# Reciprocal roots by a GpSimd power, and new instruction lists, in a cross-attention and expert kernel

## The reference

```python
x = x + xcond(layernorm(x), ctx, ctx, k_length)      # 8 heads of 16 channels; softmax over 256 keys,
                                                     # scores scaled by SCALE * log(k_length)
x = x + ffn(layernorm(x), w_router, w_fc, w_proj)    # x_flat: (1024, 256)
# layernorm(v) = (v - mean(v)) / sqrt(var(v) + 1e-5), over the last axis
# ffn: logits = x_flat @ w_router.T; the better of 2 experts is chosen, weighted by its softmax
#      h = x @ w_fc[e].T (1024 hidden); a = leaky(h, 0.5) ** 2; out = a @ w_proj[e].T
```

## Time and profile before

| | |
|---|---|
| median of three runs | 172.73 us |
| span of the profiled execution | 170.4 us (the page gives no other time of it) |
| TensorE busy | 161.4 us (95%) |
| VectorE busy | 129.2 us (76%) |
| ScalarE busy | 97.0 us (57%) |
| GpSimd busy | 58.6 us (34%) |
| chain that ended last, by engine | PE 75%, DVE 11%, waits not shown 4%, SP's queue 3%, ACT 3%, DMA 2% |

### The profile page before, as it was taken

One profiled execution on the slowest core, in us unless ns is written; L12 is line 12 of the kernel. 1 busy time (PEld: TensorE's weight loads), 2 busy tenths in 40 slices (PEclk: granted clock), 3 DMA queues, 4 the chain that ended last, 5 costly groups with the idle time before them and its releaser, 6 DMA issues.

```text
span 170.4 us, 4075 instructions
## 1 busy us (share of the span) xinstructions
PE 161.4 (95%) x1494; PEld 139.9 (82%) x1494; DVE 129.2 (76%) x301; ACT 97.0 (57%) x181; POOL 58.6 (34%) x68
## 2 busy tenths in 40 slices
PE   7998887899999989999989999999999999999992
PEld 7986745487698869896978798969879999999991
DVE  7799987999898999995999867953179875056442
ACT  4444979558659956957346526943794065335220
POOL 7331544630322420372521260405023253136330
PEclk9999999999999999999999999999999999999999
DMA  4577857794468054004501460002010000010001
GB/s 120 167 241 246 259 190 233 217 292 126 143 229 251 3 161 120 14 19 139 174 0 62 125 189 4 0 0 67 0 62 0 4 0 0 4 61 0 0 4 62
DMA packets 18883, 16.98 MB, mean 100 GB/s; under 512 B 1776, under 2 KB 18672, under 8 KB 18864
## 3 DMA queue, kind: packets, MB, share of 16 engines
q1 hardware_dynamic: 18144, 16.00, 30.3%
q10 hardware_dynamic: 720, 0.73, 1.5%
HBM read 8.72 MB, written 1.05 MB: 57 GB/s over the span
## 4 chain that ended last, share of the span: by engine, by line
PE 75%; DVE 11%; issue 4%; SPq 3%; ACT 3%; DMA 2%; DVEq 0%; ACTq 0%
PE hp L1358 25%; PE ops L1388 22%; PE pv L1342 6%; PE stp L1318 6%; PE ops L1273 5%; DVE negm L813 5%; PE snp L1265 3%; DMA x_raw<-x 2%; ACT probs L514 2%; DVE a_lo L921 2%; PE ops L1376 2%; PE pv L1376 1%; PE stp L1324 1%; PE pv L1398 1%; PE snp L1301 1%
## 5 line engine op out<-in xcount | busy, mean ns | idle before, releaser
L378 POOL TENSOR_TENSOR a_buf<-l_buf 128x512 f32<-128x512 f32 x32 | 35.7, 1119 | 77.8 <-DVE a_lo L921 44.6
L514 ACT ACTIVATE probs<-stp,scale_b 128x1024 f32<-128x1024 f32 x30 | 33.4, 1114 | 14.8 <-PE stp L1318 11.3
L1358 PE MATMUL hp<-xt_hi,wfc_hi 128*128 128x256 f32 x128 | 37.2, 291 | 0.0
L813 DVE TENSOR_REDUCE negm<-snp 128x4 f32<-128x1024 f32 x28 | 34.1, 1218 | 3.6 <-PE snp L1265 3.4
L1358 PE MATMUL hp<-xt_hi,wfc_lo 128*128 128x256 f32 x128 | 35.8, 279 | 0.0
L1358 PE MATMUL hp<-xt_lo,wfc_hi 128*128 128x256 f32 x128 | 35.7, 279 | 0.0
L522 ACT ACTIVATE l_buf<-hp 128x512 f32<-128x512 f32 x32 | 18.8, 594 | 23.7 <-PE hp L1358 17.0
L921 DVE TENSOR_TENSOR a_lo<-a_buf,a_hi 128x512 fp32r<-128x512 f32 x32 | 26.2, 831 | 7.6 <-ACT a_hi L529 6.2
L1358 PEld LDWEIGHTS hp<-xt_hi,wfc_hi 128*128 128x128 f32 x128 | 24.0, 188 | 2.1 <-issue 1.0
L1388 PE MATMUL ops<-wproj_hi,a_hi 128*128 128x256 f32 x112 | 23.6, 292 | 0.5 <-DVE wproj_lo L953 0.5
L1358 PEld LDWEIGHTS hp<-xt_hi,wfc_lo 128*128 128x128 f32 x128 | 24.1, 188 | 0.0
(11 more groups left out here) (112 smaller groups left out, 237.2 us busy)
## 6 DMA issues: line engine op xcount, KB each, us to landing
k_st<-k_hi SPq DMA_DIRECT2D x16, 128.0 KB, 2.1
wfc_raw<-w_fc_t SPq DMA_DIRECT2D x8, 256.0 KB, 4.4
wproj_raw<-w_proj_t SPq DMA_DIRECT2D x8, 256.0 KB, 3.5
q_st<-q_hi SPq DMA_DIRECT2D x14, 128.0 KB, 2.1
x_raw<-x SPq DMA_DIRECT2D x8, 128.0 KB, 3.0
k_st<-k_lo SPq DMA_DIRECT2D x8, 128.0 KB, 2.4
v_raw<-ctx_t SPq DMA_DIRECT2D x8, 128.0 KB, 2.6
x_keep<-x SPq DMA_DIRECT2D x8, 128.0 KB, 2.7
```

The source lines that it names most:

```text
L378: pool.tensor_tensor(a_buf[d % 2][:, :, :], l_buf[d % 2][:, :, :], l_buf[d % 2][:, :, :], ALU.mult).then_inc(s_a, 1)
L514: act.activation(probs[g][:, :, :, :], pair[:, :, :].rearrange("p e (c n) -> p e c n", c=KC), ACT.Exp, scale=scale_b[:, b:b + 1]).then_inc ...
L813: dve.tensor_reduce(negm[b % 2][:, :, :, g].rearrange("p c e -> p e c"), pair[:, :, :].rearrange("p e (c n) -> p e c n", c=KC), AX.X, ALU. ...
L1358: last = pe.matmul(hp[:, d % 2, half], wfc[w][:, kc, c * P:(c + 1) * P], xt[:, kc, :], start=(c % 2 == 0 and kc == 0 and w == 0 and xt is ...
```

## The change

The reciprocal root is now one GpSimd instruction per batch: (variance + eps) to the power -0.5, with a column `expo` that VectorE fills with -0.5 at the head. The logarithms, exponentials and Newton steps are gone. The lists of all five engines are written in another order. ScalarE's table load stands at the head of its list in both kernels.

```diff
-            def x_ln(b):
-                act.wait_ge(s_xvar, b + 1)
-                act.activation(xln[b % 2][:, :], xvar[b % 2][:, :], ACT.Ln, scale=-2.0).then_inc(s_xln, 1)
-
-            def x_rstd(b):
-                act.wait_ge(s_xln, b + 1)
-                act.activation(xrs[b % 2][:, :], xln[b % 2][:, :], ACT.Exp, scale=-0.5).then_inc(s_xrs, 1)
...
-                if stage == 0:
-                    dve.wait_ge(s_rs_, b + 1)
-                    dve.scalar_tensor_tensor(n1[:, :], rs[:, :], rs[:, 0:1], var[:, :], ALU.mult, ALU.mult).then_inc(s_n1_, 1)
-                else:
-                    dve.wait_ge(s_n1_, b + 1)
-                    dve.scalar_tensor_tensor(sc[:, :], n1[:, :], 1.5, rs[:, :], ALU.add, ALU.mult).then_inc(s_sc_, 1)
...
+            def x_scale(b):
+
+                j = b % 2
+                if b == 0:
+                    pool.wait_ge(s_expo, 1)
+                pool.wait_ge(s_xvar, b + 1)
+                wait(pool, s_qf, b - 1)
+                pool.tensor_tensor(xsc[j][:, :], xvar[j][:, :], expo[:, :], ALU.pow).then_inc(s_xsc, 1)
+
+            def y_scale(b):
+
+                j = b % 2
+                pool.wait_ge(s_yvar, b + 1)
+                wait(pool, s_x2n, b - 1)
+                pool.tensor_tensor(ysc[j][:, :], yvar[j][:, :], expo[:, :], ALU.pow).then_inc(s_ysc, 1)
...
-                    dve.tensor_scalar(var[:, :], mv[:, 1:2], EPS, -0.5, ALU.add, ALU.mult).then_inc(s_var_, 1)
+                    wait(dve, s_used, b - 1)
+                    dve.tensor_scalar(var[:, :], mv[:, 1:2], EPS, None, ALU.add).then_inc(s_var_, 1)
...
             load_x(sp, 0)
             load_x(sp, 1)
+            load_weights(sp, 0, 0)
+            load_weights(sp, 0, 1)
+            load_v(1)
             stack_k(sp, 0, 0)
```

More of the change, by code:

```diff
@@ L72, in build @@
         xst, xmv, xvar = two("xst", [P, 6]), two("xmv", [P, 2]), two("xvar", [P, 1])
-        xln, xrs, xn1, xsc = (two(n, [P, 1]) for n in ("xln", "xrs", "xn1", "xsc"))
+        xsc, expo = two("xsc", [P, 1]), sb("expo", [P, 1])
         q_f = two("q_f", [P, DIM])
@@ L87, in build @@
         yst, ymv, yvar = two("yst", [P, 6]), two("ymv", [P, 2]), two("yvar", [P, 1])
-        yln, yrs, yn1, ysc = (two(n, [P, 1]) for n in ("yln", "yrs", "yn1", "ysc"))
+        ysc = two("ysc", [P, 1])
         dot_out = sb("dot_out", [P, DIM])
@@ L383, in _ @@
             zero_k(0)
[L384 to L389, removed]
             fill_sel(0)
             fill_sel(1)
+            x_scale(0)
+            x_scale(1)
+            zero_nm(0)
             split_k(1)
+            split_k(2)
+            fill_v(0)
+            zero_k(1)
+            place_v(0)
+            fill_v(1)
+            place_v(1)
+            zero_nm(1)
+            x_scale(2)
             split_w(0, 0)
-            place_v(0)
-            split_k(2)
+            x_scale(3)
             split_w(0, 1)
             split_w(0, 2)
+            make_zeros()
             split_w(0, 3)
+            x_scale(4)
+            x_scale(5)
             split_k(3)
-            place_v(1)
+            split_k(4)
+            y_scale(0)
+            place_v(2)
+            place_v(3)
+            y_scale(1)
+            split_k(5)
             split_w(0, 4)
@@ L427, in _ @@
             square(1, 5)
+            y_scale(4)
+            y_scale(5)
+            place_v(7)
             square(1, 6)
@@ L741, in _, with fill_expo, moments @@
         def _(dve):
-            def moments(stage, b, src, st, mv, var, s_st_, s_mv_, s_var_):
+            def fill_expo():
+                dve.memset(expo[:, :], -0.5).then_inc(s_expo, 1)
+            def moments(stage, b, src, st, mv, var, s_st_, s_mv_, s_var_, s_used):
                 if stage == 0:
@@ L1078, in _ @@
-            x2_sum(2)
-            row_max(4, 1)
-            square_lo(0, 1)
-            x2_moments(2, 0)
+            q_part_lo(5)
+            split_max_lo(3)
+            x_moments(6, 1)
+            split_w_lo(1, 0)
+            split_w_lo(1, 1)
+            split_w_lo(1, 2)
+            split_w_lo(1, 3)
+            split_w_lo(1, 4)
+            square_lo(0, 0)
+            x_moments(6, 2)
+            pv_turn(2)
+            row_max(4, 0)
+            den_inverse(2)
+            attention_out(2)
@@ L1082, in _ @@
+            row_max(4, 1)
+            attention_turn(2)
+            x2_sum(2)
+            neg_logit(0)
+            x_moments(7, 0)
+            neg_abs(0)
+            row_max(4, 2)
+            square_lo(0, 1)
+            row_max(4, 3)
+            split_max_hi(4)
+            split_max_lo(4)
+            x2_moments(2, 0)
+            x_moments(7, 1)
             x2_moments(2, 1)
             coef_sum(0)
-            row_max(4, 2)
+            x2_moments(2, 2)
+            x_moments(7, 2)
@@ L1484, in _ @@
             scores_qk(3, 1)
+            x_transpose(0)
             warm(48)
-            x_transpose(0)
             scores_kq(2, 2)
+            warm(49)
             scores_qk(3, 2)
-            warm(49)
             ffn1(0, 0)
@@ L1494, in _ @@
             values(2, 0)
-            values(2, 1)
             ffn1(0, 2)
```

760 lines of the change are left out of this document (330 added, 430 removed).

## The result

| | before | after |
|---|---|---|
| median, us | 172.91 (172.65 to 173.48, four runs) | 177.53 (175.75 to 179.67, four runs) |
| profiled execution, us | span 170.4 | 177.23, span 175.4 |
| TensorE, VectorE, ScalarE, GpSimd busy, us | 161.4, 129.2, 97.0, 58.6 | 163.1, 129.2, 93.2, 67.7 |

The changed kernel is slower, by a ratio of 1.0231 (95% interval 1.0176 to 1.0285). The forecast had the sign right and was 2.9 us too low; the median lies 0.5 us above its range. By the ratio the time would be 176.9 (1.0231 times 172.91), just inside it.

What follows compares the result with a forecast made beforehand. Latency was taken to bound the kernel up to 41.94 us, TensorE's fixed stock of work after that. Head +1.0, middle +0.3, shape changes +1.6 and waits -1.0 summed to +1.9, so 174.6 us, range 171.7 to 177.0.

Steps and rivals of the forecast that it cites:

- the one from q to the last maximum: Opening: q 1.63 us late, less savings, makes batch 0's last maximum 1.04 late, priced +1.0 us (+0.6 to +5.2).
- two savings: Opening: q_lo of batch 1 moved ahead of the first maxima saves 0.35 us, one warm fewer between permutations 0.24.
- Constants: Start of q: constants land later because SP issues weights and v first; taken as 0.1 us, bounds 0 and 2.5.
- The ISA row: Start of q: a row before GpSimd's first two-input instruction costs between 0 and 0.98 us; taken as 0.1.
- The power: Start of q: one GpSimd power on one column, estimated at 0.35 us from the sizes of other GpSimd instructions.
- the rival of 1.28: Opening: the power takes as long as GpSimd's dearest instruction, adding 1.4 us, so 176.0 us; chance 0.12.
- the code load: Opening: the first power pays its own code load, 175.5 us or more, about 180 by the skill's figure; chance 0.04.
- The place that was priced: Middle, batch 2: first to second scores about 2.2 us, second to fourth maximum 3.9; the middle's net was +0.3.
- The waits: Long stretch: TensorE's named waits of 0.49 us (split maxima) and 0.54 (weight piece) both regained, -1.0 us.
- The changes of shape: Long stretch: 16 more TensorE tile shape changes at 0.10 us each, +1.6 us, bounds 0 and 3.0.
- Faster: Opening: VectorE's throughput is the limit there, so removed instructions give back 1.9 us; 171.8 us, chance 0.18.
- no change: Whole kernel: head +0.6, middle 0, shape changes +0.8, waits -1.0, together +0.4, so 173.1 us; chance 0.14.

Runs made afterwards that it cites:

- c: Changed kernel with ten more warm calls (20 multiplications of zeros) ahead of the first permutation; 175.81 us, ratio 1.019 to the kernel before.
- a: Changed kernel with SP's two early weight pieces and early piece of v put behind batch 0's k stack transfers; 173.79 us, ratio 1.0064 to the kernel before.
- d: Changed kernel with SP's early loads moved back, first power ahead of the casts and q_part_lo(0) ahead of q_normalise(1); 174.76 us, ratio 1.0085.
- e: Changed kernel with loads back, power ahead of casts, VectorE's batch 0 statistics ahead of k's low part, q_f(0) before batch 1's statistics; 174.46 us, ratio 1.007.
- t: Changed kernel with early loads moved back and the first half of values right ahead of the second in batches 2 to 7; 176.53 us, ratio 1.0215.
- m: Changed kernel with early loads moved back and TensorE's list up to the first projection in the order of the kernel before; 175.78 us, ratio 1.0161.
- p2: Kernel before, old lists with the power, plus batch 4's max_transpose one chunk later and two weight pieces' low parts earlier on VectorE; 171.0 us, ratio 0.9864.
- p: Kernel before with its own lists, only the reciprocal roots replaced by GpSimd powers, the first ahead of the casts; 171.84 us, ratio 0.9937.
- b: Changed kernel with the first power ahead of GpSimd's two casts and q_part_lo(0) ahead of q_normalise(1) on VectorE; 175.06 us, ratio 1.0098.
- q: New lists on all engines with the old reciprocal root (logarithm, exponential, Newton pair), no power on GpSimd; 183.08 us, ratio 1.0492 to the kernel before.
- pi: Old lists with the power, without the seven warm calls between batch 0's second and third scores; 172.39 us, ratio 0.9951 to the kernel before.
- pl: Old lists with the power, but SP issues two weight pieces and one of v ahead of batch 0's k stacks; 172.79 us, ratio 0.9972.

## Why the prediction was right in sign and wrong in size

**Slower: right, for a reason that is half of the true one.** The power does wait for the constants and the casts. But q's lateness was expected to pass through at its own size, and it did not. Against the landmarks the head was priced 3.66 too low, the middle 0.82 too low and the long stretch 1.32 too high. That the time came out near the upper bound and not far above it is luck: the third miss hid part of the first two.

**The step that failed is the one from q to the last maximum.** It put q 1.63 late (it was 2.27, 7.31 for 5.04) and let the maxima follow at their old pace, less two savings, "1.04 late". It took TensorE's pace as given and never asked what TensorE does while q is late. It idles, and the granted clock falls to the lower of its two levels (1.2 for 2.4 GHz). The head came out at +4.66. The runs, read one after the other by the first transpose, part it so (one profiled execution each, and a step's size depends on this order; c's added zeros are not in a): 2.76 the clock (changed kernel to c), 0.61 the early loads (c to a), 0.22 the power behind the casts (a to d), 0.37 statistics behind k (d to e), 0.70 left over the kernel before, by the row at ScalarE's copy of q.

The Trainium skill, TensorE: Matmul & The Clock Gate, Part 1, "What's actually happening", says that the slow clock is the default state and that activity releases the throttle. The stage rows above agree: 0.77 and then 0.71 behind the idle time, and c, where zeros fill it, has 1.00 in both stages up to 20 us. They do not show when idle time is enough: t's 1.55 us and m's 2.01 were followed by no fall. Read against the planned gap ahead of the permutation, that rule would have given this rival.

**The terms of q's start.** Constants: +0.70 in place of 0.1 (5.92 for 5.22). The bound of 2.5 had the mechanism, transfers that share the engines; a shows it. What the step left out is that the k stacks share them too (4.66 us in the chain; 2.1 before). The ISA row: 0.04 (6.68 to 6.72) for 0.1. The power: 0.55 for 0.35; the rival of 1.28 falls, and so does the code load.

The Trainium skill's 6 us for a first call (GPSIMD Engine Reference, section 2.1 "Instruction dispatch") do not show here: the first power starts 0.04 us after the cast ends.

**Middle: +1.12 for +0.3.** The place that was priced came out as priced. The rows that answer to the earlier trace rows:

```profile
32.23 0.39 PE L1257 MATMUL hp<-q_st,k_st 64*128 64x256 f32 x2 [0.74 <-ACT probs L529]
...
32.90 0.50 PE L1204 MATMUL snp<-k_st,q_st 64*128 64x256 f32 x4
33.33 1.07 PE L1281 MATMUL pv<-probs,v_one 128*32 128x256 f32 x16
...
35.19 0.50 PE L1204 MATMUL snp<-k_st,q_st 64*128 64x256 f32 x4
...
35.73 1.23 DVE L787 TENSOR_REDUCE negm<-snp 128x4 f32<-128x1024 f32 x1 [0.15 <-PE snp L1204]
...
39.63 1.23 DVE L787 TENSOR_REDUCE negm<-snp 128x4 f32<-128x1024 f32 x1 [0.23 <-PE snp L1204]
```

First to second scores 2.29 (forecast 2.2), second to fourth maximum 3.90 (forecast 3.9). What was missed is ahead of it: `scores_kq(1, 2)` now stands before the first scores of batch 2 and waits 0.74 for the softmax (before, those scores themselves waited 0.69 for their stack), and from the second `max_transpose` to those scores it takes 3.99 in place of 3.53. Another 0.43 went between the first and the second `max_transpose` (10.21 for 9.78).

**Long stretch: -0.72 for +0.6.** By the last matmuls it took 123.75 us, under the 124 that the prediction named as a sign of being wrong. The waits: both regained, as forecast, and p2 shows that such waits are worth their size; the new one at 73.44 took most of it back in this execution and is absent in a. The changes of shape: no +1.6. With the named waits taken out and each half of `values` counted as a call, the spacings between calls sum to 27.6 us after and 27.8 before (from the matmuls' start times). The rows were read rightly, but a pair of halves was taken as one block without a cost inside. In before a pair took 2.04 us (44.43 to 46.47): its second half starts 0.37 after the last block of the first, 0.22 in t, where a pair takes 1.86. That the 0.15 between them is a wait for its softmax is likely and not shown. Apart the halves take 2 x 1.00. Spacings inside the second projection's chunks sum to 0.73 us less, which is as much as the whole stretch gained; why is open.

**ScalarE's and VectorE's saved work** was counted only at two named waits. p shows that the change of the root is worth 1.0 us even where those stay; that the saved work is the reason is not shown.

**The rivals.** Faster and no change fall for the changed kernel. p's 171.84 equals the faster case's 171.8 by coincidence: that case shortened the opening by 0.9, and p's first projection starts at 42.42 for 41.94. Nothing in the prediction had the clock.

## What to carry to other kernels

Before pricing a delay on a latency path, look at what TensorE does meanwhile: if it idles, ask for its clock, and count instructions queued behind the idle time at the lower rate, fillers first. Give the first transfers of a kernel to what its first matmuls need; here 640 KB of weights and v, issued first, held up the constants and the k stacks. Change an operation and an instruction order in two steps: here the operation gained 0.6% and the order lost 3%.

## What the runs showed of the hardware that was not expected

- The granted clock fell during or right behind waits of TensorE of 1.91 us (changed kernel), 1.34 (b), 1.23 (m) and 3.16 (q), and not behind 0.87 (a), 1.18 (pi), 1.55 (t) or 2.01 (m, ahead of 17.93). In c waits of 0.73 and 0.81 in a row were followed by a fall; in a one of 0.74 and two later ones of 0.47 and 0.68 were not.
- One kernel's executions differ in this. The mean granted clock is 0.99 or less in four of four runs of the changed kernel, five of ten of pi, four of nine of b, one of ten of a and none of eight of p. Idle time makes a fall more likely; these rows give no rule for when.
- The clock column does not show the start: in the changed kernel 26 multiplications take 5.34 us from 1.07 on, 0.21 each, under a granted clock given as full.
- A power on one column takes GpSimd 0.55 us in the median of the changed kernel, 0.94 at most, and 0.60 to 0.66 as p's and pl's first one.
- 640 KB issued ahead of them took the three k stacks of batch 0 from 2.1 us each to between 3.7 and 4.7 from issue to landing.
